# An attention and FFN block on one core: a prologue reordered by need, weight tasks moved within the first FFN step, and rope's turned half kept in PSUM

## The reference, cut to what matters

```python
x = x + attention(layernorm(x))      # 16 heads; latent q (192) and kv (64), rope on 64 columns, causal
x = x + ffn(layernorm(x))            # weights are lut[idx] with a table of 16 values; silu(gate) * up, then down
x = x + state_space(layernorm(x))    # xp = x W_in, dt = softplus(xp W_dt + b), scan over time, W_out
x = x + ffn(layernorm(x))            # the same FFN weights
# in the attention, for each head:
q_pe   = rope(q_c @ wq_rope.T)       # o1 = x1*cos - x2*sin ; o2 = x1*sin + x2*cos
scores = (q_nope . k_nope + q_pe . k_rope) * scale
```

## Time and profile before

| what | value |
|---|---|
| median of 3 runs | 856.2 us (856.1 to 857.96) |
| the profiled execution | 857.25 us |
| its span in the trace | 855.2 us |
| PE busy | 763.8 us, 89% |
| DVE busy | 677.6 us, 79% |
| ACT busy | 610.7 us, 71% |
| POOL busy | 503.2 us, 59%, none after 581.4 us |

### The profile page before, as it was taken

How to read it: one execution, slowest core, us unless ns; L and a number is a source line. 1 busy time by engine, 2 the same in 40 slices (tenths; PEclk the granted TensorE clock), 3 DMA queues, 4 the chain that set the end, 5 groups by cost and what they waited for, 6 DMA issues and landing times.

```text
span 855.2 us, 15308 instructions
## 1 busy us (share of the span) xinstructions
PE 763.8 (89%) x4556; PEld 652.6 (76%) x4556; DVE 677.6 (79%) x2216; ACT 610.7 (71%) x1500; POOL 503.2 (59%) x543
## 2 busy tenths in 40 slices
PE   4767988898989899998899999999898999999998
PEld 3656767787877687876777888877787887887987
DVE  3676879898879999888989899896756778777643
ACT  2455888888888888888888899996515575665232
POOL 0599999999999999999999999981000000000000
PEclk9796999999999999999999999999989999999999
DMA  9800000000000000000000100000000000000000
GB/s 245 256 1 1 1 1 2 1 2 2 2 1 2 1 1 2 2 1 2 1 2 1 38 2 1 2 1 1 1 1 1 1 1 2 1 1 25 26 26 25
DMA packets 15377, 14.53 MB, mean 17 GB/s; under 512 B 5792, under 2 KB 14432, under 8 KB 15040
## 3 DMA queue, kind: packets, MB, share of 16 engines
q1 hardware_dynamic: 13792, 11.41, 4.6%
q0 software_dynamic: 624, 2.12, 0.8%
q10 hardware_dynamic: 880, 0.04, 0.1%
HBM read 11.46 MB, written 2.10 MB: 16 GB/s over the span
## 4 chain that ended last, share of the span: by engine, by line
PE 59%; DVE 15%; ACT 12%; issue 12%; DMA 0%; DVEq 0%; SPq 0%; ACTq 0%
PE bank L615 12%; PE bank L617 11%; PE bank L616 11%; PE bank L1496 4%; ACT prob L798 4%; ACT prob L818 3%; PE bank L1510 2%; PE bank L1513 2%; DVE pt_lo L1149 2%; ACT pt_hi L827 2%; PE bank L1523 2%; PE bank L580 2%; PE bank L1525 2%; DVE bias_m L1097 1%; PE bank L1470 1%
## 5 line engine op out<-in xcount | busy, mean ns | idle before, releaser
L746 POOL TENSOR_SCALAR hot<-raw_gu,lut 128x256 f32<-128x256 int32 x165 | 192.9, 1169 | 16.7
L752 POOL TENSOR_TENSOR total<-total,hot 128x256 f32<-128x256 f32 (+1 forms) x238 | 172.9, 726 | 19.9
L1097 DVE CUSTOM_DVE_ANT_0 bank<-bank,mask 128x128 f32<-128x128 f32 (+3 forms) x256 | 126.1, 493 | 38.6 <-issue 36.5
L798 ACT ACTIVATE prob<-bank,bias_m 128x128 f32<-128x128 f32 (+3 forms) x256 | 136.1, 532 | 23.9 <-DVE bias_m L1097 23.2
L1149 DVE TENSOR_TENSOR pt_lo<-bank,pt_hi 128x512 fp32r<-128x512 f32 x160 | 108.9, 681 | 10.2 <-ACT pt_hi L827 10.0
L1496 PE MATMUL bank<-ident,prob 128*128 128x128 f32 x640 | 98.6, 277 | 14.9 <-ACT prob L818 10.3
L818 ACT ACTIVATE prob<-prob,rden 128x128 f32<-128x128 f32 (+3 forms) x224 | 105.4, 536 | 6.0 <-DVE rden L1132 5.5
L615 PE MATMUL bank<-kt_hi,qt_hi 128*128 128x128 f32 (+3 forms) x256 | 89.6, 350 | 19.8 <-DVE xt_lo L589 5.0
L827 ACT CAST pt_hi<-bank 128x512 fp32r<-128x512 f32 x160 | 93.5, 585 | 13.9 <-PE bank L1513 8.8
L746 POOL TENSOR_SCALAR hot<-raw_dn,lut 128x256 f32<-128x256 int32 (+1 forms) x90 | 97.2, 1080 | 9.1
L1496 PEld LDWEIGHTS bank<-ident,prob 128*128 128x128 f32 x640 | 72.9, 140 | 31.9 <-ACT prob L818 16.7
(11 more groups left out here) (207 smaller groups left out, 2103.0 us busy)
## 6 DMA issues: line engine op xcount, KB each, us to landing
x<-in_L_attn_a_x_dram SPq DMA_DIRECT2D x4, 512.0 KB, 7.3
wo_nat<-in_L_attn_a_wo_dram SPq DMA_DIRECT2D x1, 2048.0 KB, 13.6
out_dram<-x SPq DMA_DIRECT2D x16, 128.0 KB, 1.8
wqu<-in_L_attn_a_wq_up_dram SPq DMA_DIRECT2D x2, 768.0 KB, 9.0
wqr<-in_L_attn_a_wq_rope_dram SPq DMA_DIRECT2D x4, 192.0 KB, 7.3
raw_dn<-in_L_ffn_down_idx_dram POOLq DMA_DIRECT2D x1, 688.0 KB, 10.1
raw_gu<-in_L_ffn_gate_idx_dram POOLq DMA_DIRECT2D x1, 640.0 KB, 7.4
raw_gu<-in_L_ffn_up_idx_dram POOLq DMA_DIRECT2D x1, 640.0 KB, 7.9
```

The source lines that it names most:

```text
L746: nc.gpsimd.tensor_scalar((hot if v else total)[:, 0:n], raw[:, c:c + n], float(v), lut[:, v:v + 1], ALU.is_equal, ALU.mult).then_inc(lut_ ...
L752: nc.gpsimd.tensor_tensor(dst, total[:, 0:n], hot[:, 0:n], ALU.add).then_inc(lut_sum, 1)
L798: nc.scalar.activation(prob[:, n % 2, h, 0:w], bank[2 + h % 2][:, 0:w], ACT.Exp, bias=bias_m[:, n % 2, h:h + 1], scale=-1.0, accum_out=den ...
L1097: nc.vector.tensor_tensor_reduce(out=bank[2 + h % 2][:, 0:w], in0=bank[2 + h % 2][:, 0:w], in1=mask[:, TB * P - w:TB * P], scale=1.0, scal ...
```

## The change

- **Prologue.** The N and R tasks are ordered so that the four that heads 0 to 7 need come first (`Q_TASKS`); the RMS steps of the first batch stand ahead of all low parts on DVE; features 0 and 1 and slot 0 (with `q_up(0)`) run before the other four tasks, and feature 2 behind them. The R tasks get banks 4 and 5.
- **Statistics of batches 1 to 3.** `rest_stats` spreads them: 12 `bn_stats` between the V tasks, the aggregation and 11 Newton steps between the stages of slot 3, the four `at_norm(1, t)` in slot 4. The transposes of batch 1 move from slot 3 to slots 4 and 5, into `bank[7]`.
- **Rope.** `q_rot` is gone. The two sine products are written back into `bank[0]`, to columns 0 to 63 of each head, which `q_copy` has read by then. The sum reads them from there, so `q_up(n+1)` now waits for all four instructions of `rope_q(n)`.
- **POOL.** `GC = GT * DIM // 8 = 352`.
- **First FFN step.** L tasks come first, S tasks after them; the two tasks for W_in and W_out stand behind the transposes of the next input, and `t_dt_in` between the two halves of `ffn_down`.

```diff
-        q_rot = r2("q_rot", [P, G, ROPE], F32)
-        GC = GT * DIM // 11
+        GC = GT * DIM // 8
+        R_TASKS = [(qr_dup, 1, t_rope(p, k), 4 + p) for k in range(2) for p in range(2)]
+        Q_TASKS = N_TASKS[0:2] + R_TASKS[0:2] + N_TASKS[2:4] + R_TASKS[2:4]
+        L_TASKS = [(lut_sum, gu_sums + dn_sums, t_dn(k), 4 + k) for k in range(3)]
+        S_TASKS = [(ssm_in, 64, t_wdt(), 7), (ssm_in, 64, t_ssm(0), 2), (ssm_in, 64, t_ssm(2), 3),
+                   (ssm_in, 64, t_dt_in(), 2)]
+        TASKS = D_TASKS + Q_TASKS + W_TASKS + V_TASKS + G_TASKS + L_TASKS + S_TASKS
...
+        def rest_stats(k):
+            e, tiles = nc.vector, slice(TB, BATCH * TB)
+            if k < REST_TILES:
+                if k % TB == 0:
+                    e.wait_ge(x_in_s[1 + k // TB], 16)
+                e.bn_stats(at_stats[:, TB + k, :], x[:, TB + k, :]).then_inc(at_bn, 1)
+            elif k == REST_TILES:
...
+            else:
+                rsqrt_step(k - REST_TILES - 1, at_ref, RSQRT + 2, at_v[:, tiles], at_r[:, tiles], at_t[:, tiles])
...
-                nc.vector.tensor_tensor(q_rot[:, :, 0:half], raw[:, :, half:ROPE], s0, ALU.mult).then_inc(q_rope, 1)
-                nc.vector.tensor_tensor(q_rot[:, :, half:ROPE], raw[:, :, 0:half], s1, ALU.mult).then_inc(q_rope, 1)
+                nc.vector.tensor_tensor(turned[:, :, 0:half], raw[:, :, half:ROPE], s0, ALU.mult).then_inc(q_rope, 1)
+                nc.vector.tensor_tensor(turned[:, :, half:ROPE], raw[:, :, 0:half], s1, ALU.mult).then_inc(q_rope, 1)
                 dve.wait_ge(q_rope, k + 3)
-                nc.vector.tensor_tensor(q, q, q_rot[:, :, :], ALU.add).then_inc(q_rope, 1)
+                nc.vector.tensor_tensor(q, turned, q, ALU.add).then_inc(q_rope, 1)
...
-                free_after(pe, q_rope, 4 * (b * UNITS + n) - 1)
+                free_after(pe, q_rope, 4 * (b * UNITS + n))
...
+                    if b == 0 and s == 3 and k <= RSQRT:
+                        rest_stats(REST_TILES + k)
+                    if b == 0 and s == 4 and k < TB:
+                        at_norm(1, k)
+                    if b == 0 and s in (4, 5) and k == 11:
+                        dve_xt_part(1, s - 4, bank[7])
...
-                pe_tasks(pe, L0 + 1, L1)
-                weights(L0 + 3)
+                weights(L0 + 2)
                 pe_xt(ffn_xt(1))
-                weights(L1)
-                ffn_down(0, None)
+                pe.wait_ge(hf_s, FT)
+                pe_tasks(pe, S0 + 1, S1 - 1)
+                weights(S0 + 1)
+                ffn_down(0, None, lambda: pe_tasks(pe, S1 - 1, S1))
```

More of the change, by code:

```diff
@@ L871, in _ @@
             act_tasks(act, D0, N0)
-            down_copy(0, 0)
-            down_copy(0, 1)
+            for t in range(TB):
+                down_copy(0, t)
             act.wait_ge(const_in, 16 * 7)
@@ L877, in _ @@
             act.wait_ge(qn_ready, 2)
[L878 to L883, removed]
+            act_tasks(act, N0, N1)
+            feature_high(0, 0)
+            feature_high(0, 1)
+            act_slot(0, 0, None)
+            act_tasks(act, N1, W0)
+            feature_high(0, 2)
             nc.scalar.activation(a_neg[:, :], a_neg[:, :], ACT.Exp).then_inc(a_exp, 1)
-            for s in range(LEAD):
+            act_tasks(act, *early_tasks(0))
+            for s in range(1, LEAD):
                 act_slot(s, 0, None)
                 act_tasks(act, *early_tasks(s))
-                if s == 3:
-                    act_xt(1)
+                if s in (4, 5):
+                    act_xt_part(1, s - 4, bank[7])
             for b in range(BATCH - 1):
@@ L1162, in add_output, with early_dve @@
                     dve_x_add(b, tile_of(n), bank[7])
+            def early_dve(k0, k1):
+                for k in range(k0, k1):
+                    dve_tasks(dve, k, k + 1)
+                    if V0 <= k < G0:
+                        for j in range(REST_TILES * (k - V0) // (G0 - V0), REST_TILES * (k + 1 - V0) // (G0 - V0)):
+                            rest_stats(j)
             def dve_slot(s, b, nb, early=(0, 0)):
@@ L1223, in dve_slot @@
                     split_values(nb)
+            for k in range(1 + RSQRT + TB):
+                token_step(k, 0)
             dve.wait_ge(qn_ready, 2)
[L1226 removed]
+            dve_tasks(dve, N0, N1)
+            feature_low(0, 0)
+            feature_low(0, 1)
             dve.wait_ge(tables_in, 16 * 3)
[L1228 removed]
+            for k in range(1 + RSQRT + TB, TOKEN_STEPS):
                 token_step(k, 0)
[L1230 to L1232 removed]
+            dve_slot(0, 0, None, (N1, W0))
+            feature_low(0, 2)
             split_values(0)
@@ L1235, in _ @@
             nc.vector.tensor_scalar(a_neg[:, :], a_neg[:, :], -1.0, None, ALU.mult).then_inc(a_ready, 1)
-            for s in range(LEAD):
+            early_dve(*early_tasks(0))
+            for s in range(1, LEAD):
                 dve_slot(s, 0, None, early_tasks(s))
[L1238 to L1245, removed]
             for b in range(BATCH - 1):
@@ L1519, in project @@
                 pe.wait_ge(o_lo_s, 1 + b * UNITS + n + 1)
+                if b == 0 and n == 0:
+                    wait_xt(pe, 1)
                 if g == 0:
@@ L1646, in output_projection, with ffn_down @@
                         last.then_inc(so_mm, 1)
-            def ffn_down(k, si):
+            def ffn_down(k, si, inside=None):
                 for pair in range(0, TB, 2):
+                    if pair and inside is not None:
+                        inside()
                     if pair and si is not None:
```

122 lines of the change are left out of this document (65 added, 57 removed).

## The result

The changed kernel takes 866.69 us in the median of four runs (866.47 to 868.12), the kernel before 856.15 (854.24 to 857.96): a ratio of 1.0127, 95% interval 1.0102 to 1.0152. It is slower by 10.5 us, where 3.0 were forecast. The profiled execution is 9.5 us longer in its span, 864.7 instead of 855.2.

A forecast was written before the change was run, and what follows sets the result against it. PE, busy 89% of the span, was taken as the bound, with the engine ending each PE gap deciding there. Prologue -0.5, release +10.3, relief -3.0, POOL +0.5 and FFN -4.3 made +3.0: 859.2 us, range 851 to 864.5.

The forecast's parts named there:

- Rope, the later release: In the attention, q_up waits for rope's fourth instruction; each slot later by 0.61 less its margin: +10.3, bounds 1.4 to 14.2.
- light slots: Attention slots 20-23, 36-39 and 52-55, where PE has no other gap worth the name: 5.3 us of the later release.
- token slots: Attention slots with token steps (11-13, 27-29, 43-45), where PE was idle before q_up: 3.9 us by margin, 0.4 taken.
- wide slots: Attention slots with the widest scores (16-19, 32-35, 48-51), where DVE runs without a gap up to the next rope: 4.6 us.
- Rope, the relief: In the attention, rope's sum with one operand in PSUM is no longer lengthened by POOL's adds: -3.0, between -1 and -5.8.
- Prologue: Up to slot 7: first row_max 5.3 us earlier, mostly given back in slots 3 to 7: -0.5, bounds -5 to +3.
- head start: In the prologue, q_up(0) starts near 33.1, 6.3 us earlier, spent by the first V task; DVE reaches first row_max 5.3 earlier.
- POOL: +0.5 forecast: Chunks of 352 columns end POOL's work near 519, but its longer adds delay instructions on DVE: +0.5, between -0.5 and +1.5.
- First FFN step: In step 0 of the FFN, ffn_down starts earlier and its first half likely runs at 2.4 GHz: -4.3; slow clock -2.6.
- shifts go round in all slots: Rival, late and slow: all margins count, 14.2, and first FFN half stays at 1.2 GHz: sum +8.6, 864.8; chance 0.1.
- PE takes it up: Rival: PE absorbs the later release elsewhere, 1.4 instead of 10.3, sum -5.9, 850.3; chance 0.2.
- the prologue keeps its 5.3: Rival: the spread steps fall wholly into DVE's gaps, -3.8 instead of -0.5, sum -0.3, 855.9; chance 0.2.

The follow-up runs named there:

- the kernels with short POOL: Three kernels in which POOL decodes two table entries only: old release 841.32 us, later release 859.32, later release with the turned half in PSUM 858.15.
- rope_part: The kernel before with the whole rope edit, turned half in PSUM and later release, POOL chunks of 256 columns: 868.60 us, ratio 1.0166.
- release_alone: The kernel before with q_up waiting for the fourth rope instruction instead of the third, q_rot kept in SBUF: 870.97 us, ratio 1.0204.
- prologue_and_ffn: The changed kernel with rope, release and POOL chunks as before, so new prologue and new FFN order only: 854.67 us, ratio 0.9987.
- pool_chunks: The kernel before with POOL chunks of 352 columns instead of 256 and nothing else: 857.92 us, ratio 1.0026.
- short_pool_old: The kernel before with POOL decoding two table entries only, done at 92 us, old release: 841.32 us, ratio 0.9836.
- short_pool_release: The kernel before with POOL decoding two table entries only and q_up waiting for the fourth rope instruction, q_rot in SBUF: 859.32 us, ratio 1.0044.

## Why the prediction was right and wrong

The direction, and the mechanism that set it, were right; the size was not, and the time of 866.69 us fell outside the range of 851 to 864.5. In the profiles the miss is 6.5 us (+9.5 instead of +3.0): attention +5.2, prologue +3.1, the end of the attention -0.8, first FFN step -1.0. By its own steps:

1. **Rope, the later release: mis-sized, 13.5 instead of 10.3.** The light slots came as forecast. The step that failed is "in the token slots ... 3.9 us by margin, of which I take 0.4": measured are 3.1 less 1.2 given back, 1.9. DVE's spare time between `scores(3)` and `row_max(3)` absorbed half of the shift, not nine tenths. I saw a gap on one edge and took it for slack in the whole round. The wide slots cost 0.7 more, slots outside the three groups 0.8. Three small readings do not change this: all margins of slots 8 to 63 come to 14.5 and not 14.2, line 1111 took up to 0.425 and not 0.420, and of the fourteen long sums one lies across a compare of POOL and not an add. The rule itself (0.61 less the margin, going round) is shown by the kernels with short POOL; its upper bound, 14.2, was nearer than the value taken.

2. **Rope, the relief: 2.0 instead of 3.0 in the profiles**, with an uncertainty larger than the difference. The sum is never held any more, as forecast. Release and relief together made +11.6 where +7.3 was forecast.

3. **Prologue: +2.6 instead of -0.5.** The head start (5.2) was right to 0.1, and "slots 3 to 7 also get the later release, 1.5" measured 1.3 in rope_part, 1.6 in release_alone and 1.8 with short POOL. The step that failed is "of which DVE's own gaps in these slots take up some 2", which left 3.3: measured are 5.6 without the release (prologue_and_ffn against before, slots 3 to 7). With PE's gaps filled in both orders 4.1 of them remain, so DVE's gaps take up 1.2 of the 5.3 and not 2. Taking 2.0 us of steps off DVE took 1.9 off the stretch, with the clock a little better, which fits. The other 1.5 is the clock, as far as the fill held it: it costs the new order 3.1 (35.3 against 32.2) and the old one 0.7 to 1.6 (28.8 to 29.7 against 28.1). The prediction named a clock of 0.50 as something that would prove it wrong, but costed the clock only up to slot 0 and in the FFN step.

4. **POOL: +0.5 forecast**, between 0 and +4 by the runs. Its bound of +1.5 was too low if pool_chunks is taken at its own ratio. Open.

5. **First FFN step: -5.3 instead of -4.3**, a little beyond the bound of -5.2, with the clock at 2.4 GHz as I held likelier. That this matches is in part luck: the forecast took the slow clock of the kernel before for a fixed property, and four of seven executions of the old order did not have it; against those the gain is 2.7.

6. **The reference.** The sum was made on one execution, whose attention stretch is the lowest of ten of the same code, by 1.4 against their mean. That is part of the 13.0 in the table of the result. The other way round, its `q_up(8)` at 102.04 is the latest of five executions with the old prologue and the old release (99.45 to 102.04), and its FFN step had the slow clock.

Of the rivals, the third ("shifts go round in all slots", 864.8) was nearest, with chance 0.1: its 14.2 is near the 13.5 measured, but the other half of it, a slow first FFN half, did not happen. The first, PE takes it up, is excluded by release_alone. The second, the prologue keeps its 5.3, is excluded by prologue_and_ffn. The 0.8 us between `q_up(63)` and the FFN appears in all kernels with the later release (41.4 to 41.6 instead of 41.8 to 42.2), but also in short_pool_old and pool_chunks (41.4), which have the old release; its cause stays open.

## What to carry to other kernels

Where a buffer is handed back on the chain's own round, read the hand-over's margin in every period and price a later release at its full sum: a gap on one edge of the loop is slack only as far as the whole round closes it, and an experiment with a neighbour silenced shows it to 0.1 us. Freeing an engine early gives nothing if the work spread behind it opens gaps in the next one, above all when PE then runs at half its clock. Where a forecast prices a slow clock that one profile of the kernel before shows, take more profiles of it first: one execution may pay a price that the next does not. Of this change's parts, one was worth keeping; measured alone it was visible at once.

## What the hardware showed that I had not expected

**POOL's hold on DVE reaches the end time.** Silencing POOL after 92 us took some 14 us off the kernel (ratio 0.9836, 0.9805 to 0.9867; 841.32 against 854.67), 11.3 of them in the attention stretch against the mean of ten, while DVE's excess over its shortest durations fell from 27.5 to 7.8. In the prediction POOL was a matter of three microseconds. The sum with both operands in SBUF took up to 0.99, and up to 1.11 with 352 columns; with one operand in PSUM 0.43 at most. All 13 sums of the kernel before that an add of POOL held end 0.28 after that add: the sum waits for the add to be over. The Trainium skill, "SBUF — State Buffer", section "Who interferes with whom", has this rule: a VectorE instruction with two SBUF inputs contends with a GpSimd instruction that reads SBUF, one with at most one SBUF input and outside the two-port modes doesn't. For the sum the traces agree.

**PSUM as a source costs the sum nothing here**: 425 ns in the mean with one operand from PSUM (rope_part), 430 ns (median 426) with both from SBUF and POOL silent (short_pool_release). As a destination it adds 9 ns to a product of 128 columns (288 against 279). The 65 ns more that the Trainium skill, "VectorE: DVE Perf Modes", section "The TRN2 errata — SBUF-src ops pay a fixed extra latency per instruction", gives a source in PSUM don't show in these runs.

**Idle transposes buy clock.** 24 of them, 3.2 us of work that nobody reads, raised the granted clock from 0.55 and 0.50 to 1.00 between 74 and 84 us and shortened the kernel: 851.22 against 854.67 us, on different chips (ratios 0.9945 and 0.9987; 0.9959 when measured again). The old order got no such proof: its own fill held the clock only in part.

**The same gaps do not always cost the clock.** In seven executions with gaps of 1.8 us at the same place of the first FFN step, the granted clock behind them was 0.50 in three and 1.00 in four, worth 2.6 us.
